# Bi-WKV gate and FFN on one core: the FFN's results of blocks 1 to 7 added up in DRAM by GpSimd's accumulating transfers

## The chip, the core and the metric

One core of a Trainium2 chip runs the whole kernel. The time is in device microseconds. Before the change it is 1723.0 us, the median of three runs (1722.13 to 1724.81).

## The reference

`x` and `fside` are (4, 1024, 1024), `cond` is (4, 256), all float32.

```python
r, k, v = x, fside, fside
tf = sigmoid(sum(time_emb)); decay = exp(-exp(w)) * (0.5 + 0.5 * tf)
ek = exp(min(k, 30)); ekv = ek * v
nf, df, nb, db = ...            # scans of ekv and ek over the sequence, forward and backward
base = sigmoid(r) * (nf + nb - ekv + euk * v) / max(df + db - ek + euk, 1e-8)
mix = base * (0.8 + 0.2 * tf)
h = mix @ W1.T                  # 4096 hidden columns
a = gelu(clip(round(h / 0.1)) * 0.1)
out = x + a @ W2.T
```

## The kernel before

The output is computed in eight blocks of 512 rows (`BLOCKS`), held transposed: eight tiles of 128 features by 512 rows (`CT` = `DT` = 8). A block has 8 hidden units `s` of 512 columns (`STEPS`) and 8 output tiles `d`. While TensorE works on block n, ScalarE and VectorE make the gate of block n + 1 (`tile_group`, and the four `part`s that `mix` calls in `chained_block`), and check the weights: 64 checks, each a load of 512 KB, a conversion to int8 on ScalarE (`check_i8`, L1258) and a comparison on VectorE (`check`, L1832); a check's load waits for the check before it (`load_check`, L524). Sixteen of them fall in block 7.

Block 0 multiplies plainly. Blocks 1 to 7 multiply in a scheme with 7 products instead of 8: an operand is cut in 2 x 2 quadrants, and the result's four quadrants are built up in PSUM banks by products named 1 to 7. ScalarE's `seed` (L1171) copies product 1 from one bank to the next, `spill_p5` (L1180) puts product 5 in `sp5`, and VectorE's `seed_u4` (L1714) sets up the bank for products 7 and 3: TensorE's `products_73` and `y_73` wait for it (`s_u4`). The hidden units use `products_15`, `products_73`, `products_26`, `product_4` (L810). The output of hidden units 0 to 3 is made in the same way in the middle of the block, in two parts `e` of four tiles: `y_15`, `y_73`, `y_26`, `y_4` (L875). Its results are quadrants `(e, c)`, c = 0 to 3, of 128 x 512. The order on TensorE there is: `y_15(0)`, `y_26(0)`, `y_15(1)`, `y_73(0)`, `y_26(1)`, `y_4(0)`, `products_15(5)`, `y_73(1)`, `products_26(5)`, `y_4(1)`. The output of hidden units 4 to 7 follows at the block's end, plainly, tile by tile (`output`, L956; the last tile of block 7 in two halves, `output_end`, L972).

Each engine's order is written out by hand, in `chained_block` of ScalarE and of VectorE and in `ffn_block` of SyncE. An engine that waits for a semaphore holds all that is behind it.

The results of blocks 1 to 7 go through four buffers `xy` of 128 x 512 in float32:

- Middle of the block: SyncE loads a quadrant of `x` (`load_quad`), VectorE adds the quadrant of PSUM to it (`y_quad`, L1734; for c = 3 also `sp5` before it, L1750), SyncE stores the sum in the DRAM array `y_part` (`store_quad`).
- End of the block: SyncE loads a tile of `y_part` (`residual`, L485), VectorE adds the tile of PSUM (`result`, L1812), SyncE stores it in `out` (`store`, L508). Two buffers take loads, two take stores. The last tile's halves are added by `result_end` (L1820, L1823).

Weights come through a ring of eight slots of 512 KB (`ring_load`, L457) on SyncE's queue, in line with all else that SyncE does. GpSimd issues the transfers that convert or copy weights, all in block 0 and before it (L717 to L728).

After the last check VectorE adds up the verdicts, one product on TensorE (L1028) makes a flag of them, and each engine reads it.

Of the kernel before, what the change touches and what calls it, by code (L numbers as in the profile page):

```python
# [5 lines left out]
P = 128  # L6
ALU = mybir.AluOpType
# [31 lines left out]
def adaln_ffn_kernel(nc, x, fside, cond, w, u, w1, w2, out):  # L39
# [22 lines left out]
    with ExitStack() as ctx:  # L62
# [12 lines left out]
        y_part = nc.dram_tensor("y_part", [BLOCKS, DT, P, T], F32).ap()  # L75
# [189 lines left out]
        s_y5 = sem("s_y5")  # L265
        s_xq = [sem(f"s_xq{k}") for k in range(4)]
        s_yq = [sem(f"s_yq{k}") for k in range(4)]
# [56 lines left out]
        def w1_pair(s, h):  # L324

            return (s // 2 + 2 * h, s % 2) if s < SPLIT else (s, h)

# [106 lines left out]
        def _(sp):  # L434
# [39 lines left out]
            def residual(n, d):  # L474
                k, uses = d % 2, DT // 2 * n + d // 2
                if uses > 0:
                    sp.wait_ge(s_res[k], uses)
                src = x[n % BLOCKS // 2, 1 - n % 2, d]
                if 0 < n < BLOCKS:
                    src = y_part[n, d]  # L480
                    sp.wait_ge(s_yq[2 * k], 16 * (2 * (n - 1) + d // 4 + 1))
                    sp.wait_ge(s_yq[2 * k + 1], 16 * (2 * (n - 1) + d // 4 + 1))
                    if d < 2:
                        sp.wait_ge(s_yq[k], 16 * 2 * n)
                sp.dma_start(x_in[:, k, :], src).then_inc(s_x[k], 16)  # L485

            def quad(dram, e, c):

                return dram[4 * e + c // 2:4 * e + 4:2, :, H * (c % 2):H * (c % 2 + 1)].rearrange("i p t -> p i t")

            def load_quad(n, e, c):
                if e == 1:
                    sp.wait_ge(s_yq[c], 16 * (2 * (n - 1) + 1))
                elif c < 2:
                    sp.wait_ge(s_res[c], DT // 2 * n)
                else:
                    sp.wait_ge(s_store[c - 2], 16 * DT // 2 * n)
                sp.dma_start(xy_quads[:, c, :, :], quad(x[n // 2, 1 - n % 2], e, c)).then_inc(s_xq[c], 16)

            def store_quad(n, e, c):  # L500
                done = (s_y11, s_y12, s_y21, s_c22)[c]
                sp.wait_ge(done, part_y(n, e) + 1 if c == 3 else 2 * (n - 1) + e + 1)
                sp.dma_start(quad(y_part[n], e, c), xy_quads[:, c, :, :]).then_inc(s_yq[c], 16)

            def store(n, d):
                k, uses = d % 2, DT // 2 * n + d // 2
                sp.wait_ge(s_res[k], uses + 1)
                sp.dma_start(out[n % BLOCKS // 2, 1 - n % 2, d], y_out[:, k, :]).then_inc(s_store[k], 16)  # L508

            def store_end(n, d):  # L510
                sp.wait_ge(s_resend, 1)
                sp.dma_start(out[n // 2, 1 - n % 2, d][:, 0:H], y_out[:, 1, 0:H]).then_inc(s_store[1], 16)
                sp.wait_ge(s_res[1], DT // 2 * n + d // 2 + 1)
                sp.dma_start(out[n // 2, 1 - n % 2, d][:, H:T], y_out[:, 1, H:T]).then_inc(s_store[1], 16)
# [62 lines left out]
            def ffn_block(n):  # L577
# [8 lines left out]
                for s in range(1, SPLIT + 1):  # L586
                    ring_load(3)
                    if s == 1:
                        store(n - 1, DT - 2)
                        store(n - 1, DT - 1)  # L590
# [4 lines left out]
                    if s == SPLIT:  # L595
                        for c in range(4):
                            load_quad(n, 0, c)
# [6 lines left out]
                store_quad(n, 0, 0)  # L604
                ring_load(3)
                load_quad(n, 1, 0)
# [4 lines left out]
                store_quad(n, 0, 3)  # L611
                store_quad(n, 0, 1)
                ring_load(2)
                store_quad(n, 0, 2)
                load_quad(n, 1, 3)
                load_quad(n, 1, 1)
                store_quad(n, 1, 0)
                ring_load(2)
                load_quad(n, 1, 2)
# [5 lines left out]
                store_quad(n, 1, 3)  # L625
                store_quad(n, 1, 1)
                load_check(at + 2 if nxt else at + 7)
                ring_load(2)
                store_quad(n, 1, 2)
# [10 lines left out]
                residual(n, 0)  # L640
                residual(n, 1)
# [4 lines left out]
                store(n, 0)  # L646
                residual(n, 2)
                ring_load(2)
                store(n, 1)
                residual(n, 3)  # L650
# [4 lines left out]
                store(n, 2)  # L655
                residual(n, 4)
# [4 lines left out]
                store(n, 3)  # L661
                residual(n, 5)
                load_check(at + 5 if nxt else at + 15)
                ring_load()
                store(n, 4)
                residual(n, 6)
                ring_load()
                store(n, 5)
                residual(n, 7)
# [7 lines left out]
            store(BLOCKS - 1, DT - 2)  # L677
            store_end(BLOCKS - 1, DT - 1)
            for k in range(2):
                sp.wait_ge(s_store[k], 16 * (DT // 2 * BLOCKS + k))  # L680
# [25 lines left out]
            with sp.If(needs_general > 0):  # L706
                for m in range(BLOCKS):
                    general_block(m)
                for k in range(2):
                    sp.wait_ge(s_store[k], 16 * (DT // 2 * 2 * BLOCKS + k))  # L710

        @block.gpsimd
        def _(pool):
# [9 lines left out]
            for s in range(STEPS):  # L723
                pool.wait_ge(s_y, 2 + s)
                for r, h, k in ((WP1, 0, 0), (WP2, 0, 1), (WP4, 1, 1)):
                    g, pair = w1_pair(s, h)
                    pool.wait_ge(s_w1cast[g], 16)
                    pool.dma_start(w1s[s][:, r, :, :], w1_quads[g][:, pair, :, k, :]).then_inc(s_w1copy[s], 16)  # L728
            for d in range(DT):
                pool.wait_ge(s_w2cast[d], 16)  # L730
            for s in range(STEPS):
                pool.wait_ge(s_w1copy[s], 16 * 3)

        @block.tensor
        def _(pe):
# [79 lines left out]
            def bank_free(n, s, q):  # L815
# [7 lines left out]
                if s == 0 and n > 1:  # L823
                    for k in range(2):
                        pe.wait_ge(s_res[k], DT // 2 * (n - 1) + 2)
                if s == 1 and n > 1:
                    for k in range(2):
                        pe.wait_ge(s_res[k], DT // 2 * n)
# [134 lines left out]
            def output_end(n, d):  # L963
# [3 lines left out]
                pe.wait_ge(s_res[0], DT // 2 * n + 2)  # L967
# [62 lines left out]
            def general_block(m):  # L1030
                n = BLOCKS + m
                pe.wait_ge(s_out, CT * (n + 1))
                for s in range(STEPS):
                    pe.wait_ge(g_w[s % 2], 16 * (DT * m + s // 2 + 1))
                    for j in range(FPS):
                        if FT * m + FPS * (s - 2) + j + 1 > 0:
                            pe.wait_ge(g_q, FT * m + FPS * (s - 2) + j + 1)
                        if s == 0 and j in (0, 3):
                            pe.wait_ge(s_res[j % 2], DT // 2 * n)
# [4 lines left out]
                for d in range(DT):  # L1044
                    pe.wait_ge(g_w[d % 2], 16 * (DT * m + STEPS // 2 + d // 2 + 1))
                    pe.wait_ge(s_res[d % 2], DT // 2 * n + d // 2)
# [16 lines left out]
        def _(act_e):  # L1063
# [186 lines left out]

            def check_i8(at):
# [53 lines left out]
            def chained_block(n, nxt, g0, at):  # L1305
# [42 lines left out]
                act_hi(n, SPLIT, 1)  # L1348
                seed(part_y(n, 1))
                check_i8(at if nxt else at + 3)  # L1350
                spill_p5(part_y(n, 1))
                if nxt:
                    tile_group_between(g0 + 3)
                check_i8(at + 1 if nxt else at + 4)
# [4 lines left out]
                else:  # L1359
                    check_i8(at + 5)  # L1360
                quantise11(n, SPLIT + 1)

# [39 lines left out]
                check_i8(at + 2 if nxt else at + 10)  # L1402
                if nxt:
                    tile_group_between(g0 + 7)
                    operands_hi(n + 1, 1)
                check_i8(at + 3 if nxt else at + 11)
                check_i8(at + 4 if nxt else at + 12)
                if nxt:
                    reciprocal(g0 + 7, s_gate, g0 + 8)
                    operands_hi(n + 1, 2)  # L1410
                    if n + 2 < BLOCKS:
                        tile_group(g0 + CT)
                    operands_hi(n + 1, 3)
                check_i8(at + 5 if nxt else at + 13)
                if not nxt:
                    check_i8(at + 14)
                    check_i8(at + 15)

# [54 lines left out]
        def _(dve):  # L1473
# [256 lines left out]
            def y_quad(n, e, c, ps, done, flag_of):  # L1730

                dve.wait_ge(done, part_y(n, e) + 1)
                dve.wait_ge(s_xq[c], 16 * (2 * (n - 1) + e + 1))
# [465 lines left out]
```

## Time and profile before

| | |
|---|---|
| median of three runs | 1723.0 us |
| the profiled execution | 1722.96 us |
| its span | 1720.6 us |
| granted TensorE clock, mean | 0.991 of full speed |
| TensorE busy | 1647.8 us, 96% |
| VectorE busy | 1298.0 us, 75% |
| ScalarE busy | 936.3 us, 54% |
| GpSimd busy | 24.7 us, 1% |
| moved by DMA | 376.97 MB, queues busy 67.4% of 16 engines |

The profiled execution is one run; its span leaves out what lies ahead of the first and behind the last instruction, 2.4 us. A matmul's mean time is from its start to its modelled end, and matmuls overlap: busy time over count is their pace. Blocks 1 to 7 begin at about 288, 490, 693, 897, 1102, 1304 and 1508 us. A part of the chain called "issue" is time in which an engine waited for nothing that the profile shows.

### The profile page before, as it was taken

To read this page: it belongs to the slowest core of one execution; us is meant where nothing else is said; L and a number is where in the kernel's file an instruction comes from. 1 tells how busy PE (TensorE), PEld (TensorE's weight loads), DVE (VectorE), ACT (ScalarE), POOL (GpSimd) and SP (SyncE) were. 2 spreads that over 40 slices of the span, in tenths; PEclk is the share of its full clock that TensorE was granted. 3 is DMA by queue.
4 is the path that set the end of the run, shared out by engine and by line. 5 is a ranking of instruction groups with operands and counts; after the bars stand their busy time and mean duration, and the time that the engine had idled before them with its cause. 6 is when DMAs were issued, how large, how long until landed. Compare 5 with 4: busy or idle time off the path is not lost. (4 is left out here: it accounts for less than half of the span.)

```text
span 1720.6 us, 30810 instructions
## 1 busy us (share of the span) xinstructions
PE 1647.8 (96%) x12258; PEld 1200.1 (70%) x12258; DVE 1298.0 (75%) x1795; ACT 936.3 (54%) x1461; POOL 24.7 (1%) x44
## 2 busy tenths in 40 slices
PE   1699999999999999999999999999999999999997
PEld 0244445888578884888758885688857887488864
DVE  8988896887779769788697877888787876955232
ACT  3578332765656564673836646475555646365141
POOL 0000110000000000000000000000000000000000
PEclk9799999999999999999999999999999999999999
DMA  8979885587375865668466684757737585565754
GB/s 238 245 176 281 307 305 166 180 275 238 135 275 167 273 204 207 217 193 285 152 222 227 221 262 137 265 184 268 242 133 272 172 283 178 199 213 187 247 181 152
DMA packets 153461, 376.97 MB, mean 219 GB/s; under 512 B 15328, under 2 KB 44256, under 8 KB 152800
## 3 DMA queue, kind: packets, MB, share of 16 engines
q1 hardware_dynamic: 150624, 351.86, 61.0%
q0 software_dynamic: 2688, 23.07, 5.9%
q8 instruction: 99, 1.62, 0.4%
q14 instruction: 50, 0.41, 0.1%
HBM read 347.61 MB, written 67.11 MB: 241 GB/s over the span
## 5 line engine op out<-in xcount | busy, mean ns | idle before, releaser
L810 PE MATMUL ps<-mo,w_ring 128*128 128x256 f16 x6272 | 695.4, 273 | 5.9 <-DVE q L1726 4.0
L810 PEld LDWEIGHTS ps<-mo,w_ring 128*128 128x128 f16 x6272 | 612.9, 98 | 83.7 <-issue 7.9
L956 PE MATMUL ps<-act,w_ring 128*128 128x512 f16 x1760 | 383.3, 379 | 0.0
L875 PE MATMUL ps<-act,w_ring 128*128 128x256 f16 x3136 | 348.1, 273 | 0.0
L875 PEld LDWEIGHTS ps<-act,w_ring 128*128 128x128 f16 x3136 | 306.3, 98 | 36.0
L956 PEld LDWEIGHTS ps<-act,w_ring 128*128 128x128 f16 x1760 | 172.2, 98 | 203.2
L1768 DVE SCALAR_TENSOR_TENSOR act<-a,act 128x1024 f16<-128x1024 f32 x72 | 87.8, 1221 | 86.4 <-ACT act L1232 86.4
L1222 ACT ACTIVATE a<-q 128x1024 f32<-128x1024 int16 x124 | 131.0, 1057 | 7.0 <-DVE act L1768 2.0
L1171 ACT ACTIVATE ps<-ps 128x512 f32<-128x512 f32 x70 | 40.7, 581 | 169.0 <-PE ps L810 113.7
L751 PE MATMUL ps<-mo,w_ring 128*128 128x512 f16 x256 | 66.4, 427 | 56.3 <-DMA w_ring<-w_half 33.6
L1714 DVE SCALAR_TENSOR_TENSOR ps<-sp,ps 128x512 f32<-128x512 f32 x70 | 48.5, 692 | 85.3 <-issue 37.3
L942 PE MATMUL ps<-act,w_ring 128*128 128x512 f16 x512 | 110.7, 379 | 0.0
L1258 ACT ACTIVATE q<-tt 128x1024 int8<-128x1024 f32 x48 | 50.5, 1051 | 109.7 <-DMA tt<-in_w_dram 109.7
L751 PEld LDWEIGHTS ps<-mo,w_ring 128*128 128x128 f16 x256 | 27.1, 108 | 95.1 <-issue 47.1
L942 PEld LDWEIGHTS ps<-act,w_ring 128*128 128x128 f16 x512 | 50.1, 98 | 60.4
L1616 DVE SCALAR_TENSOR_TENSOR ND<-EE,bonus,ND 128x1024 f32<-128x1024 f32 x64 | 81.8, 1279 | 1.6
L1596 DVE TENSOR_TENSOR_SCAN ND<-decay,back,ND 128x512 f32<-128x512 f32 x64 | 81.9, 1280 | 0.6
L1600 DVE TENSOR_TENSOR_SCAN ND<-decay,back,ND 128x512 f32<-128x512 f32 x64 | 81.7, 1276 | 0.0
L1107 ACT ACTIVATE RCP<-ND 128x512 f32<-128x512 f32 x64 | 40.3, 630 | 67.1 <-DVE ND L1620 64.7
L1232 ACT ACTIVATE act<-a 128x1024 f16<-128x1024 f32 x72 | 75.9, 1054 | 1.5
L1779 DVE TENSOR_TENSOR tt<-a 128x1024 f32<-128x1024 f32 x28 | 34.3, 1225 | 54.2 <-ACT a L1222 54.2
L1204 ACT ACTIVATE q<-ps 128x512 int16<-128x512 f32 x56 | 33.3, 595 | 70.1 <-PE ps L810 69.9
(129 smaller groups left out, 1730.1 us busy)
## 6 DMA issues: line engine op xcount, KB each, us to landing
w_ring<-w1s SPq DMA_DIRECT2D x168, 512.0 KB, 4.6
w_ring<-w_half SPq DMA_DIRECT2D x130, 512.0 KB, 5.2
w_ring<-w2s SPq DMA_DIRECT2D x56, 512.0 KB, 5.1
tt<-in_w_dram SPq DMA_DIRECT2D x48, 512.0 KB, 5.6
V<-in_fside_dram SPq DMA_DIRECT2D x64, 256.0 KB, 5.7
R<-in_x_dram SPq DMA_DIRECT2D x64, 256.0 KB, 5.9
w_half<-in_w_dram POOLq DMA_DIRECT2D x16, 1024.0 KB, 9.5
xy<-in_x_dram SPq DMA_DIRECT2D x64, 256.0 KB, 5.0
```

The source lines that it names most:

```text
L751: mm = pe.matmul(bank[4 * (s % 2) + j][:, :], w1_ring[:, slots[2 * s + j // 2], j % 2, c, :], mix0[:, c, p, :], start=(first and p == 0), ...
L810: mm = pe.matmul(dst[:, f, :], wp_ring[:, k, r, f, q, :], mo[:, op, q, p, :], start=(fresh and f == 0 and q == 0 and p == 0), stop=(q == K ...
L875: mm = pe.matmul(dst[:, i, :], wy_ring[:, k, i, 2 * s + j, :], ao[:, s, op, j, p, :], start=(fresh and i == 0 and s == 0 and j == 0 and p ...
L942: mm = pe.matmul(y_ps[y][:, :], w2_ring[:, k, f, :], act[:, FPS * s + j, p, :], start=(h == 0 and f == 0 and p == 0), stop=(h == 1 and f = ...
L956: mm = pe.matmul(bank[d][:, :], w2_ring[:, k, FPS * (s - SPLIT) + j, :], act[:, act_at(n, s) + j, p, :], start=(s == SPLIT and j == 0 and ...
L1222: sc.activation(a32[:, 2 * h:2 * h + 2, :], src[:, s % 2, 2 * h:2 * h + 2, :], ACT.Gelu_apprx_tanh, scale=QSTEP).then_inc(s_gelu, 1)
L1232: sc.activation(act[:, f:f + 2, 0, :], a32[:, 2 * h:2 * h + 2, :], ACT.Copy, scale=ACT_SCALE).then_inc(s_ahi, 1)
L1258: sc.activation(small, full, ACT.Copy, scale=W_SCALE).then_inc(s_chki8, 1)
L1596: v.tensor_tensor_scan(DEN[:, k, :][:, ::-1], dec(b, c), DEN[:, k, :][:, ::-1], back[:, k, 1:2], ALU.mult, ALU.add).then_inc(s_dbwd, 1)
L1600: v.tensor_tensor_scan(NUM[:, k, :][:, ::-1], dec(b, c), NUM[:, k, :][:, ::-1], back[:, k, 0:1], ALU.mult, ALU.add).then_inc(s_nbwd, 1)
L1616: v.scalar_tensor_tensor(out=ND[:, k, :, :], in0=EE[:, k, :, :], scalar=bonus[:, b, c:c + 1], in1=ND[:, k, :, :], op0=ALU.mult, op1=ALU.ad ...
L1768: v.scalar_tensor_tensor(out=act[:, f:f + 2, 1, :], in0=a32[:, 2 * h:2 * h + 2, :], scalar=ACT_SCALE, in1=act[:, f:f + 2, 0, :], op0=ALU.m ...
```

## The change

`y_part` is gone. For blocks 1 to 7:

- SyncE copies `x` to `out` in DRAM, four transfers of two tiles each (`copy_x`), one in each of hidden units 1 to 4.
- ScalarE copies the quadrants 0 to 2 of each part from PSUM to an `xy` buffer (`y_quad`), and later the output tiles (`output_out`), the last tile of block 7 excepted. VectorE makes quadrant 3 from PSUM and `sp5` in one instruction (`y22`).
- GpSimd adds each buffer to `out` in DRAM by a transfer with `accum_op=ALU.add`, in the order of `event`: (0,0), (0,3), (0,1), (1,0), (0,2), (1,3), (1,1), (1,2), then the tiles. Tiles begin when all eight quadrants have landed.
- All four buffers are used in turn. Whoever fills one waits until the transfer from it has landed (`buffer_free`, `s_acc`).
- TensorE waits for ScalarE's copies (`s_ev`) before it reuses the banks of the output, where it waited for VectorE's `s_res`.
- The last tile of block 7 stays with VectorE: SyncE loads it from `out` after tile 5's transfer has landed, since it uses tile 5's buffer (`residual_end`).

```diff
+        def buffer_free(engine, n, i):
+            if added(n, i) > 0:
+                engine.wait_ge(s_acc[i % 4], 16 * added(n, i))
...
+            def copy_x(n, i):
+                sp.dma_start(out[n // 2, 1 - n % 2, 2 * i:2 * i + 2], x[n // 2, 1 - n % 2, 2 * i:2 * i + 2]).then_inc(s_xcopy, 16)
...
+            def residual_end(n, d):
+                for k in range(4):
+                    sp.wait_ge(s_acc[k], 16 * added(n, 8))
+                sp.wait_ge(s_acc[1], 16 * (added(n, 2 * DT - 3) + 1))
+                sp.dma_start(x_in[:, 1, :], out[n // 2, 1 - n % 2, d]).then_inc(s_x[1], 16)
...
+            for n in range(1, BLOCKS):
+                dram = out[n // 2, 1 - n % 2]
+                pool.wait_ge(s_xcopy, 16 * 4 * n)
+                for e, c in ((0, 0), (0, 3), (0, 1), (1, 0), (0, 2), (1, 3), (1, 1), (1, 2)):
...
+                    pool.dma_start(quad(dram, e, c), xy_quads[:, k, :, :], accum_op=ALU.add).then_inc(s_acc[k], 16)
+                for k in range(4):
+                    pool.wait_ge(s_acc[k], 16 * added(n, 8))
+                for d in range(DT if n + 1 < BLOCKS else LAST):
+                    pool.wait_ge(s_ev, DT * (n - 1) + d + 1)
+                    pool.dma_start(dram[d], xy[:, d % 4, :], accum_op=ALU.add).then_inc(s_acc[d % 4], 16)
...
-                    for k in range(2):
-                        pe.wait_ge(s_res[k], DT // 2 * (n - 1) + 2)
+                    pe.wait_ge(s_ev, DT * (n - 2) + DT // 2)
...
+            def y_quad(n, e, c):
+                i, q = event(e, c), part_y(n, e)
+                act_e.wait_ge((s_p2, s_p3, s_p4)[c], q + 1)
+                buffer_free(act_e, n, i)
+                sc.activation(xy_quads[:, i % 4, :, :], halves[4 * (q % 2) + (0, 3, 1)[c]], ACT.Copy,
+                              scale=1.0 / QUAD_SCALE).then_inc((s_y11, s_y12, s_y21)[c], 1)
+
+            def output_out(n, *tiles):
+                for d in tiles:
+                    act_e.wait_ge(s_y, y_all(n, d))
+                    buffer_free(act_e, n, DT + d)
+                    sc.activation(xy[:, d % 4, :], bank[d][:, :], ACT.Copy, scale=1.0 / ACT_SCALE).then_inc(s_ev, 1)
...
                 spill_p5(part_y(n, 1))
+                y_quad(n, 0, 1)
                 if nxt:
                     tile_group_between(g0 + 3)
+                y_quad(n, 1, 0)
+                y_quad(n, 0, 2)
                 check_i8(at + 1 if nxt else at + 4)
...
-            def y_quad(n, e, c, ps, done, flag_of):
-
-                dve.wait_ge(done, part_y(n, e) + 1)
```

ScalarE, middle of block 2, before (L1258 is the check's conversion, L1171 a seed, L1180 a spill, L1090 to L1113 a tile of the next block's gate):

```order
L1171 ACTIVATE ps<-ps 128x512 [waits s_q21,s_p1]
L1258 ACTIVATE q<-tt 128x1024 [waits s_chk,s_gelu,s_chkload]
L1180 ACTIVATE sp<-ps 128x512 [waits s_c22,s_p5]
L1125 ACT_TABLE_LOAD
L1090 ACTIVATE EE,ksum<-V 128x512 [waits s_gate,s_v1]
L1099 ACTIVATE RCP,vsum<-V 128x512 [waits s_vsq,s_out]
L1107 ACTIVATE RCP<-ND 128x512 [waits s_out,s_vsq,s_gate]
L1109 ACTIVATE RCP<-RCP 128x512 [waits s_ln]
L1113 ACTIVATE R,rsum<-R 128x512 [waits s_r1]
L1258 ACTIVATE q<-tt 128x1024 [waits s_chk,s_gelu,s_chkload]
L1171 ACTIVATE ps<-ps 128x512 [waits s_y21,s_p1]
```

and now:

```order
L1257 ACTIVATE xy<-ps 128x512 [waits s_acc0,s_p2]
L1172 ACTIVATE ps<-ps 128x512 [waits s_q21,s_p1]
L1273 ACTIVATE q<-tt 128x1024 [waits s_chk,s_gelu,s_chkload]
L1181 ACTIVATE sp<-ps 128x512 [waits s_c22,s_p5]
L1257 ACTIVATE xy<-ps 128x512 [waits s_acc2,s_p3]
L1126 ACT_TABLE_LOAD
L1091 ACTIVATE EE,ksum<-V 128x512 [waits s_gate,s_v1]
L1100 ACTIVATE RCP,vsum<-V 128x512 [waits s_vsq,s_out]
L1108 ACTIVATE RCP<-ND 128x512 [waits s_out,s_vsq,s_gate]
L1110 ACTIVATE RCP<-RCP 128x512 [waits s_ln]
L1114 ACTIVATE R,rsum<-R 128x512 [waits s_r1]
L1257 ACTIVATE xy<-ps 128x512 [waits s_acc3,s_p2]
L1257 ACTIVATE xy<-ps 128x512 [waits s_acc0,s_p4]
L1273 ACTIVATE q<-tt 128x1024 [waits s_chk,s_gelu,s_chkload]
L1172 ACTIVATE ps<-ps 128x512 [waits s_y21,s_p1]
```

The copies (L1257) of quadrants (1,0) and (0,2) stand between the tile's gate and the second conversion (L1273).

VectorE at the same place, now (L1845 is the check, L1746 `seed_u4` of part 1):

```order
L1580 TENSOR_TENSOR EE<-EE,V 128x512 [waits s_ekx]
L1608 SCALAR_TENSOR_TENSOR ND<-decay,EE 128x512 [waits s_ekv]
L1610 SCALAR_TENSOR_TENSOR ND<-decay,EE 128x512
L1586 TENSOR_TENSOR ND<-ND,RCP 128x512 [waits s_rcp0]
L1621 COPY back<-carry 128x2 [waits s_carry,s_dfwd,s_nfwd]
L1845 SCALAR_TENSOR_TENSOR tt,bad<-q,tt 128x1024 [waits s_chki8]
L1746 SCALAR_TENSOR_TENSOR ps<-sp,ps 128x512 [waits s_q12,s_p6,s_sp5]
```

Before, the sum of quadrant (1,0) stood between the check and the seed; the check was ahead of the seed then too.

ScalarE at the end of block 7, now (before, seven conversions stood here with nothing between them):

```order
L1264 ACTIVATE xy<-ps 128x512 [waits s_acc2,s_y]
L1273 ACTIVATE m_st<-m_st 128x1024 [waits s_chk,s_chkload]
L1264 ACTIVATE xy<-ps 128x512 [waits s_acc3,s_y]
L1273 ACTIVATE m_st<-m_st 128x1024 [waits s_chk,s_chkload] x2
L1264 ACTIVATE xy<-ps 128x512 [waits s_acc0,s_y]
L1264 ACTIVATE xy<-ps 128x512 [waits s_acc1,s_y]
L1264 ACTIVATE xy<-ps 128x512 [waits s_acc2,s_y]
```

Tiles 4, 5 and 6 are copied after the last conversion.

## Rows read from the trace of the kernel before

**Rows 1.** The page's busy us (share of the span) and instructions of each engine.

```profile
PE 1647.8 (96%) x12258; PEld 1200.1 (70%) x12258; DVE 1298.0 (75%) x1795; ACT 936.3 (54%) x1461; POOL 24.7 (1%) x44
```

**Rows 2.** Waits of TensorE: engine, line, who was waited for: us, times, longest us.

```profile
PE ps L810 <- DVE q L1726: 4.0, 5, 0.9
...
PE ps L810 <- ACT ps L1171: 1.7, 2, 1.4
```

**Rows 3.** Chain of waits, around the start of block 6: start us, us, what.

```profile
1313.72 5.23 DMA tt<-in_w_dram
...
1334.48 0.70 DVE q L1726
1335.17 0.14 issue
```

**Rows 4.** Groups by line: line engine op, out<-in xcount | busy us, mean ns | idle before.

```profile
L1812 DVE SCALAR_TENSOR_TENSOR xy<-ps,xy 128x512 f32<-128x512 f32 x63 | 42.9, 685 | 15.3 <-PE ps L942 8.2 <-DMA xy<-y_part 7.0
...
L1734 DVE SCALAR_TENSOR_TENSOR xy<-ps,xy 128x512 f32<-128x512 f32 x56 | 38.3, 688 | 25.5 <-PE ps L875 18.6 <-issue 3.6 <-DMA xy<-in_x_dram 2.8
...
L1750 DVE SCALAR_TENSOR_TENSOR xy<-sp,xy 128x512 f32<-128x512 f32 x14 | 9.6, 688 | 22.5 <-DMA xy<-in_x_dram 22.5
```

**Rows 5.** Timeline of TensorE, middle of block 7: start us, us, instructions.

```profile
1582.70 24.62 PE L875 MATMUL ps<-act,w_ring 128*128 128x256 f16 x224
1607.15 3.66 PE L810 MATMUL ps<-mo,w_ring 128*128 128x256 f16 x32
1610.65 7.15 PE L875 MATMUL ps<-act,w_ring 128*128 128x256 f16 x64
```

**Rows 6.** Timeline of VectorE in the same stretch.

```profile
1597.48 1.22 DVE L1832 SCALAR_TENSOR_TENSOR m_st<-m_st 128x1024 f32<-128x1024 int8 x1
...
1603.92 0.70 DVE L1714 SCALAR_TENSOR_TENSOR ps<-sp,ps 128x512 f32<-128x512 f32 x1 [1.69 <-PE ps L875]
1607.35 0.69 DVE L1734 SCALAR_TENSOR_TENSOR xy<-ps,xy 128x512 f32<-128x512 f32 x1 [2.74 <-PE ps L875]
```

**Rows 7.** Timeline of ScalarE, block 7, hidden units.

```profile
1536.75 1.05 ACT L1258 ACTIVATE m_st<-m_st 128x1024 int8<-128x1024 f32 x1
...
1540.97 0.58 ACT L1171 ACTIVATE ps<-ps 128x512 f32<-128x512 f32 x1
1541.47 1.05 ACT L1242 ACTIVATE act<-a 128x1024 f16<-128x1024 f32 x1
```

**Rows 8.** Timeline of VectorE, block 7, hidden units.

```profile
1537.83 1.23 DVE L1832 SCALAR_TENSOR_TENSOR m_st<-m_st 128x1024 f32<-128x1024 int8 x1 [1.82 <-ACT m_st L1258]
...
1538.98 0.69 DVE L1714 SCALAR_TENSOR_TENSOR ps<-sp,ps 128x512 f32<-128x512 f32 x1
```

**Rows 9.** DMA issues: out<-in, queue, xcount, KB each, median us from issue to landing.

```profile
w_half<-in_w_dram POOLq DMA_DIRECT2D x16, 1024.0 KB, 9.5
...
out_dram<-xy SPq DMA_DIRECT2D x63, 256.0 KB, 4.7
...
w1s<-w_half POOLq DMA_DIRECT2D x24, 256.0 KB, 6.4
```

**Rows 10.** The page's 40 slices of 43 us, VectorE: busy tenths.

```profile
DVE  8988896887779769788697877888787876955232
```

**Rows 11.** Timeline of GpSimd, block 0: three issues in one row.

```profile
192.03 2.09 POOL L728 DMA_DIRECT2D w1s<-w_half  x3 [40.95 <-PE ps L942]
```

**Rows 12.** Chain of waits at the program's end.

```profile
1682.30 4.71 DMA m_st<-in_w_dram
...
1711.23 2.99 DMA xy<-y_part
```

**Rows 13.** Timeline of the last 60 us, three engines.

```profile
1678.61 1.23 DVE L1832 SCALAR_TENSOR_TENSOR m_st<-m_st 128x1024 f32<-128x1024 int8 x1 [5.11 <-ACT m_st L1258]
...
1702.66 7.15 PE L972 MATMUL ps<-act,w_ring 128*128 128x256 f16 x64
...
1707.83 1.06 ACT L1258 ACTIVATE m_st<-m_st 128x1024 int8<-128x1024 f32 x1 [5.83 <-DMA m_st<-in_w_dram]
```

More of the change, by code:

```diff
@@ L264, in adaln_ffn_kernel @@
         s_y21 = sem("s_y21")
-        s_y5 = sem("s_y5")
-        s_xq = [sem(f"s_xq{k}") for k in range(4)]
-        s_yq = [sem(f"s_yq{k}") for k in range(4)]
+        s_xcopy = sem("s_xcopy")
+        s_acc = [sem(f"s_acc{k}") for k in range(4)]
+        s_ev = sem("s_ev")
         s_yend = sem("s_yend")
@@ L326, in w1_pair, with uses_of, quad, event @@
             return (s // 2 + 2 * h, s % 2) if s < SPLIT else (s, h)
+        def uses_of(n, d):
+            if n == 0:
+                return d // 2
+            return DT // 2 if n < BLOCKS else DT // 2 * (n - BLOCKS + 1) + d // 2 + d % 2
+        def quad(dram, e, c):
+            return dram[4 * e + c // 2:4 * e + 4:2, :, H * (c % 2):H * (c % 2 + 1)].rearrange("i p t -> p i t")
+        def event(e, c):
+            return ((0, 0), (0, 3), (0, 1), (1, 0), (0, 2), (1, 3), (1, 1), (1, 2)).index((e, c))
+        def added(n, i):
+            return 4 * (n - 1) + i // 4
+        def buffer_free(engine, n, i):
+            if added(n, i) > 0:
+                engine.wait_ge(s_acc[i % 4], 16 * added(n, i))
+            elif i % 4 < 2:
+                engine.wait_ge(s_res[i % 4], DT // 2)
+            else:
+                engine.wait_ge(s_store[i % 4 - 2], 16 * DT // 2)
         def quantised0(s, j):
@@ L587, in ffn_block @@
                     ring_load(3)
-                    if s == 1:
-                        store(n - 1, DT - 2)
-                        store(n - 1, DT - 1)
+                    if n == 1 and s == 1:
+                        store(0, DT - 2)
+                        store(0, DT - 1)
+                    copy_x(n, s - 1)
                     if not nxt:
@@ L732, in _ @@
                 pool.wait_ge(s_w1copy[s], 16 * 3)
+            for k in range(4):
+                pool.wait_ge(s_acc[k], 16 * (added(BLOCKS - 1, 2 * DT) - k // 3))
         @block.tensor
@@ L823, in bank_free @@
                 if s == 0 and n > 1:
-                    for k in range(2):
-                        pe.wait_ge(s_res[k], DT // 2 * (n - 1) + 2)
+                    pe.wait_ge(s_ev, DT * (n - 2) + DT // 2)
                 if s == 1 and n > 1:
-                    for k in range(2):
-                        pe.wait_ge(s_res[k], DT // 2 * n)
+                    pe.wait_ge(s_ev, DT * (n - 1))
             def products_15(n, s):
```

172 lines of the change are left out of this document (58 added, 114 removed).

## The prediction

> **What bounds the kernel now.** I read the busy shares first. TensorE is busy for 1647.8 of 1720.6 us, VectorE for 1298.0, ScalarE for 936.3 [rows 1]. So work taken from VectorE is worth something only where TensorE waits for it. The list of TensorE's waits says how much that is: in blocks 1 to 7, 4.0 us for `quantise22` on VectorE (five times) and 1.7 us for a `seed` on ScalarE [rows 2], 5.7 us together. The chain of waits shows what stands behind them: a check load of 5.23 us near the start of block 6, then some 16 us of ScalarE and VectorE work, then `quantise22`, 0.14 us later the product [rows 3]. No eviction to `xy` is in that chain. Blocks 1 to 7 thus run at TensorE's pace, and only the last microseconds of the program, where the last tile waits for a load, lie elsewhere [rows 12].
>
> **What is removed.** VectorE loses 55 of its 63 evictions of 685 ns, the 56 quadrant sums of 688 ns become 14, and 14 additions of the spill, two per block, go [rows 4]: (55 + 42 + 14) x 0.69 = 77 us of busy time. Price on the path: 0, since the cover is TensorE and none of the waits of [rows 2] stands behind these instructions. It stays 0 also if VectorE comes earlier by that much, for `quantise22` waits for the check load and ScalarE. SyncE loses 56 loads and 56 stores of quadrants, 55 loads of partial sums and 55 stores of results, and gets 28 copies of 512 KB (four each in the stretch of hidden units 1 to 4). They stand ahead of weight loads on SyncE's queue, which run up to seven chunks of 3.5 us ahead; price 0.
>
> **What ScalarE gets.** 42 quadrants and 55 tiles, 0.50 us from start to start [rows 7], 49 us on an engine that is 54% busy. The share does not matter, the order does: each copy waits in line, and what stands behind it waits too. Two of the new waits are long. The copy of quadrant (0,1) holds ScalarE until `y_73` of part 0 is through; the next tile's exponentials then come some 6 us later, and VectorE has that much to give. The copy of quadrant (0,2) is the one that counts. It needs the end of `y_4` of part 0, and behind it stands a check conversion; VectorE's check waits for that conversion; behind the check stands `seed_u4` of part 1; and TensorE's next but one piece, `y_73` of part 1, needs that seed.
>
> I time it in block 7. `y_4` ends at 1607.15, and `y_73` starts at 1610.65 [rows 5]. An engine that waited for `y_4` starts 0.20 us after it, 1607.35 [rows 6]. Copy, to the next start: 0.50 [rows 7]. Conversion: 1.05 [rows 7], and 0.03 from its end to the check [rows 7, 8]. Check to the next start: 1.15 [rows 8]. Seed: 0.69 [rows 8]. Release of TensorE: 0.14 [rows 3]. That is 1607.35 + 3.56 = 1610.91, so TensorE waits 0.26 us. Before, the check had run at 1597.48 and the seed at 1603.92, 6.7 us ahead of its use [rows 6]. The same order stands in all seven blocks: 7 x 0.26 = **+1.8 us**. The bounds are 0 (the pieces overlap a little more) and 0.5 x 7 = 3.5.
>
> **The output tiles.** Tile 0's copy stands ahead of a tile's exponentials and holds them until the tile's product is through; VectorE, rid of its evictions there, makes that up before the next block's operands are due. The copies of tiles 6 and 7 fall in time in which ScalarE waits for the next block's first product. Price 0; if that cover is gone, TensorE would wait at the start of a block, up to 0.5 us per copy.
>
> **The buffers.** Four buffers serve 16 transfers per block. The closest reuse is of the buffer of quadrant (0,3): the end of its product is 96 of 224 matmuls into the stretch at 1582.70, 1593.2, and (1,3)'s is 3.5 us after 1610.65, 1614.1: 20.9 us. Unless a transfer takes that long, nobody waits for one. No row shows an accumulating transfer. The nearest is the one of GpSimd with the same size and a DRAM target, 6.4 us from issue to landing; the ends are a plain store of the same buffer, 4.7, and a transfer four times as large, 9.5 [rows 9]. I take 6.4. The issue costs GpSimd 0.70 us, a third of 2.09 [rows 11].
>
> A rule speaks against this. Those three issues of 2.09 us [rows 11] lie in the fifth of the 40 slices, where VectorE was 8 tenths busy [rows 10], and they are not drawn out. The Trainium skill (SBUF — State Buffer, section "SBUF: two separate sides") says that GpSimd can't write descriptors while VectorE runs an instruction in a two-port mode, and so such a transfer waits. Trace and rule do not conflict: the instructions beside these transfers have two tensor inputs, and the page names plain copies and `tensor_scalar`. If the rule bit, a transfer would be late by one VectorE instruction, about 1.2 us, which changes only the end.
>
> **The end.** Before, SyncE issued the load of check 12 only at 1682.30, since the stores of tiles 0 and 1 stood ahead of it [rows 12]; the check before it had ended at 1678.61 + 1.23 = 1679.84 [rows 13]. Now it goes there at once: the chain of checks comes 2.45 us sooner, and the last conversion starts at 1707.83 - 2.45 = 1705.38 [rows 13]. But ScalarE copies tiles 4, 5 and 6 only behind it: 1706.44, 1706.94, 1707.44. Tile 4 is ready for GpSimd at 1707.02, its issue takes 0.70, tile 5 is issued at 1707.72 and lands 6.4 later, 1714.1. The last load waits for it (same buffer), takes 2.99 as before [rows 12] and lands at 1717.1, where it landed at 1714.2. The end is the same from there: **+2.9 us**, with a transfer of 4.7 us +1.2, with one of 9.5 us +6.0. TensorE ends at 1709.8 [rows 13] and is not what ends last.
>
> The Trainium skill (DMA: Bandwidth & Descriptors, section "Anatomy of one DMA") gives 2.0 us plus the bytes over 436 GB/s; by that page my estimate for 256 KB is 2.6 us; the end would come to -0.9 instead of +2.9, and the sum to 1723.9, which is the case "hidden altogether" below. The rows have plain transfers of that size at 4.7 and more beside other traffic, so the forecast goes by them.
>
> **Sum:** 1.8 + 2.9 = +4.7 us on 1722.96, the time of the profiled execution, which is the median of the runs (1723.0) within 0.1: **1727.7 us**. The case's own range is +1.2 (no wait in the middle, 4.7 us transfers) to +9.5 (0.5 us per block, 9.5 us transfers).
>
> **Rivals.**
> - *Hidden altogether.* The 0.26 us is a difference of 3.76 and 3.50; a little overlap cancels it, and a transfer of 4.7 us leaves +1.2: 1724.2.
> - *Faster.* The waits of 5.7 us [rows 2] go, if less traffic lets the check load land sooner than 5.23 us. SyncE has fewer transfers in line, which speaks for it; that the loads right ahead of it are tile loads and weights, which stay, speaks against it. 1723.0 - 5.7 + 1.2 = 1718.5.
> - *Crowded.* GpSimd's transfers of tiles 6 and 7 fly just before the check load of the next block. The waits of [rows 3] grow with its landing one to one: 1 us later in each of six blocks gives 1727.7 + 6 = 1733.7.
> - *Slow additions,* the one that ends far on the other side. Adding means that DRAM is read, then written. From about 21 us per transfer on, ScalarE waits for a buffer at quadrant (0,2), and every further microsecond is paid in seven blocks and once at the end. At 25 us: 1723.0 + 1.8 + 7 x 3.9 + 2.9 + (25 - 6.4) = 1773.6. No row shows a 256 KB transfer near that.
>
> **How the numbers follow.** A measurement of this kernel can tell about 0.2%, 3.4 us, from no change. Chances: forecast 0.50, hidden 0.20, faster 0.12, crowded 0.10, slow additions 0.08. Of the forecast's 0.50, three tenths lie below +3.4. Slower: 0.35 + 0.10 + 0.08 = 0.53. Same: 0.15 + 0.20 = 0.35. Faster: 0.12. The range of 8 in 10 leaves out the slow additions and about half of the faster case and reaches past the crowded one: 1720 to 1737; the forecast's own range is 1724.2 to 1732.5.
>
> **What would show it.** A new wait of TensorE for VectorE's `seed_u4` at `y_73` of part 1, seven times, 0.2 to 0.5 us each; VectorE idle some 6 us before the check ahead of it, released by ScalarE; landing of 5 to 9 us for the accumulating transfers; no wait of ScalarE for one; at the end GpSimd's issue for tile 5 near 1709.5 (1707.7 plus the 1.8), the load behind it, then two half tiles. Wrong is the forecast if ScalarE waits for accumulating transfers inside the blocks, if TensorE's 5.7 us vanish, or if the last load comes before 1711.

## The result and the profile after

| | before | after |
|---|---|---|
| median of 10 runs each, in turn on one chip | 1722.92 us | 1727.99 us |
| lowest and highest | 1721.71, 1724.81 | 1725.66, 1732.71 |
| profiled execution, its span | 1722.96, 1720.6 us | 1728.37, 1726.6 us |
| ratio, 95% interval | | 1.003 (1.0022 to 1.0038) |

The kernel is 5.1 us (0.3%) slower; 4.7 had been forecast. The experiments show that the number came out right although two effects that the sum had put at 0 are missing in it. One is the crowding of the DMA engines, which costs 5.8 to 13.4 us. The other is VectorE's relief, which gives 2.4 to 10.0 us back. Each depends on whether the other is there, and both together cost 3.4 us. (The comparisons leave disturbed executions out; the held additions below had two, at 2518 and 6646 us, among ten.)

The page of the changed kernel, busy us of each engine and its DMA queues, answers to [rows 1]:

```profile
PE 1648.9 (96%) x12258; PEld 1199.1 (69%) x12258; DVE 1232.5 (71%) x1684; ACT 986.4 (57%) x1558; POOL 139.2 (8%) x155
...
q1 hardware_dynamic: 105216, 308.33, 52.8%
q0 software_dynamic: 25840, 52.18, 17.8%
```

VectorE lost 65.5 us, where 77 had been forecast: 0.59 for each of the 111 instructions taken (their durations are 0.69, and each overlaps its neighbour by 0.1); ScalarE got 50.1, 49 had been forecast. The queues of the kernel before:

```profile
q1 hardware_dynamic: 150624, 351.86, 61.0%
q0 software_dynamic: 2688, 23.07, 5.9%
```

GpSimd's queue (q0) moves 29 MB more in 111 additions and takes 307 us of the 16 DMA engines (17.8% of 1726.6) where it took 102: 1.85 us of all 16 for each addition of 262 KB. (The page counts the time that a queue's packets took. In some windows below this share comes out above 1, so packets overlap in it.) SyncE's queue (q1) needs 138 us less (61.0% of 1720.6 before, 52.8% of 1726.6 now).

The waits of TensorE in blocks 1 to 7, which answer to [rows 2] (L813 is the line of the hidden units' products, L876 that of the part products):

```profile
PEld ps L813 <- issue: 7.1, 8, 1.2
PE ps L813 <- DVE q L1758: 2.7, 3, 0.9
PEld ps L876 <- issue: 2.5, 7, 0.4
PE ps L813 <- ACT ps L1172: 2.2, 3, 1.0
```

At the starts of blocks TensorE waits 4.9 us in sum (5.7 before), and there are seven new waits at L876. The page puts these on the weight loads (PEld) and names no releaser; that it is the seed follows from the times below. The middle of block 7, timelines of TensorE, ScalarE and VectorE, answers to [rows 5] and [rows 6]:

```profile
1608.49 3.66 PE L813 MATMUL ps<-mo,w_ring 128*128 128x256 f16 x32
1612.25 7.15 PE L876 MATMUL ps<-act,w_ring 128*128 128x256 f16 x64
...
1608.69 0.60 ACT L1257 ACTIVATE xy<-ps 128x512 f32<-128x512 f32 x1 [6.39 <-PE ps L876]
1609.18 1.05 ACT L1273 ACTIVATE m_st<-m_st 128x1024 int8<-128x1024 f32 x1
...
1610.26 1.23 DVE L1845 SCALAR_TENSOR_TENSOR m_st<-m_st 128x1024 f32<-128x1024 int8 x1 [14.80 <-ACT m_st L1273]
1611.41 0.69 DVE L1746 SCALAR_TENSOR_TENSOR ps<-sp,ps 128x512 f32<-128x512 f32 x1
```

From the start of the 32 matmuls to that of the 64 it is 3.76 us, where it was 3.50: 0.26. It is 3.76 or 3.77 in all seven blocks. Copy, conversion, check and seed stand behind each other as forecast, and the 64 matmuls start 0.15 us after the seed's end at 1612.10.

The chain of waits at the end, which answers to [rows 12]:

```profile
1704.11 3.80 DMA m_st<-in_w_dram
1707.93 0.02 ACT m_st L1273
...
1708.90 0.59 ACT xy L1264
1709.48 0.28 issue
1709.77 0.54 POOL out_dram L729
1710.31 6.49 DMA out_dram<-xy
...
1716.88 3.03 DMA xy<-out_dram
1719.93 0.42 DVE xy L1833
```

The last sum starts at 1719.93 instead of 1714.24, 5.7 us later.

### The profile page after: what moved, and what is told of

Read it like the earlier page. It is cut to its first block and busy times, and to the rows that moved or that the text cites. A ratio compares the mean times of both kernels' runs of the same rounds, so it can differ in the third digit from the quotient of the medians.

```text
span 1726.6 us, 30636 instructions
## 1 busy us (share of the span) xinstructions
PE 1648.9 (96%) x12258; PEld 1199.1 (69%) x12258; DVE 1232.5 (71%) x1684; ACT 986.4 (57%) x1558; POOL 139.2 (8%) x155
## 3 DMA queue, kind: packets, MB, share of 16 engines
q1 hardware_dynamic: 105216, 308.33, 52.8%
q0 software_dynamic: 25840, 52.18, 17.8%
## 5 line engine op out<-in xcount | busy, mean ns | idle before, releaser
L813 PE MATMUL ps<-mo,w_ring 128*128 128x256 f16 x6272 | 695.1, 273 | 5.1 <-DVE q L1758 2.7
L813 PEld LDWEIGHTS ps<-mo,w_ring 128*128 128x128 f16 x6272 | 613.1, 98 | 82.5 <-issue 7.1
L876 PE MATMUL ps<-act,w_ring 128*128 128x256 f16 x3136 | 348.1, 273 | 0.7
L876 PEld LDWEIGHTS ps<-act,w_ring 128*128 128x128 f16 x3136 | 305.8, 98 | 38.4 <-issue 2.5
L724 POOL DMA_DIRECT2D out_dram<-xy x56 | 66.9, 1195 | 810.6 <-ACT xy L1257 709.6
L1746 DVE SCALAR_TENSOR_TENSOR ps<-sp,ps 128x512 f32<-128x512 f32 x70 | 48.4, 692 | 110.2 <-issue 49.4
L1273 ACT ACTIVATE q<-tt 128x1024 int8<-128x1024 f32 x48 | 50.4, 1049 | 77.0 <-DMA tt<-in_w_dram 77.0
L943 PEld LDWEIGHTS ps<-act,w_ring 128*128 128x128 f16 x512 | 50.1, 98 | 60.4
L729 POOL DMA_DIRECT2D out_dram<-xy x55 | 47.6, 883 | 544.1 <-ACT xy L1264 539.0
L1257 ACT ACTIVATE xy<-ps 128x512 f32<-128x512 f32 x42 | 24.7, 588 | 112.0 <-PE ps L876 112.0
L1845 DVE SCALAR_TENSOR_TENSOR tt<-q,tt 128x1024 f32<-128x1024 int8 x48 | 58.6, 1221 | 35.0 <-ACT q L1273 34.9
```

What stands on the lines that cost most here:

```text
L724: pool.dma_start(quad(dram, e, c), xy_quads[:, k, :, :], accum_op=ALU.add).then_inc(s_acc[k], 16)
L813: mm = pe.matmul(dst[:, f, :], wp_ring[:, k, r, f, q, :], mo[:, op, q, p, :], start=(fresh and f == 0 and q == 0 and p == 0), stop=(q == K ...
L876: mm = pe.matmul(dst[:, i, :], wy_ring[:, k, i, 2 * s + j, :], ao[:, s, op, j, p, :], start=(fresh and i == 0 and s == 0 and j == 0 and p ...
L943: mm = pe.matmul(y_ps[y][:, :], w2_ring[:, k, f, :], act[:, FPS * s + j, p, :], start=(h == 0 and f == 0 and p == 0), stop=(h == 1 and f = ...
L1845: v.scalar_tensor_tensor(out=full, in0=small, scalar=1.0 / W_SCALE, in1=full, op0=ALU.mult, op1=ALU.not_equal, accum_out=bad[:, at:at + 1] ...
```

## The experiments

All edits are made to the changed kernel. The "starts" in a sentence below are TensorE's waits for VectorE and ScalarE in the hidden units of blocks 1 to 7, in us (lines L810 to L816, by the kernel). The runs were made on three chips, each beside the kernel before, whose median was 1722.7, 1723.6 and 1722.7 us. The changed kernel itself was not run again beside them, so a difference from its 1728.0 can be off by about 1 us; the ratios to the kernel before do not suffer from this.

**ScalarE's order in the middle.**

```diff
+                check_i8(at + 1 if nxt else at + 4)
                 y_quad(n, 1, 0)
                 y_quad(n, 0, 2)
-                check_i8(at + 1 if nxt else at + 4)
```

> Only ScalarE's order in the middle of blocks 1 to 7 is changed: the check's conversion stands ahead of the copies of quadrants (1,0) and (0,2). My theory: VectorE's check and seed_u4 of part 1 come back ahead of their use, TensorE's wait of 0.26 us before y_73 of part 1 is gone in all seven blocks, and the time falls by 1.8 us from 1728.0 to 1726.2. Rival, the loss in the middle has nothing to do with this order (slower transfers, a longer block 0): the gap stays, and the time stays at 1728.0.

1724.6 us (ratio to before 1.001, 1.0001 to 1.0019): 3.4 less than with the change. The seven waits at L876 are gone, and the 3.76 us are 3.50 again in all seven blocks. The other half of the gain is open, and the two intervals are wide enough to hold 1.8 as well as 3.4. The starts of its profiled execution, the slowest with 1729.07 us, are 7.8 and so more than the changed kernel's 4.9.

```profile
PE ps L813 <- DVE q L1758: 4.3, 5, 0.9
PE ps L813 <- ACT ps L1172: 3.5, 3, 2.0
```

The next run has 3.2, and neither edit touches the start of a block: the starts vary from one execution to the next, and so does the start of block 1, which lies between 286.9 and 289.5 us in the profiled executions of this document.

**The end of block 7.**

```diff
                 output_out(n, 3)
+                if not nxt:
+                    output_out(n, 4, 5)
                 check_i8(at + 4 if nxt else at + 14)
...
                 else:
+                    output_out(n, 6)
                     check_i8(at + 15)
-                    output_out(n, 4, 5, 6)
```

> Only the last block's order on ScalarE is changed: tiles 4 and 5 are copied before check conversion 14, tile 6 before conversion 15, where all three stood behind 15. My theory: tile 5's transfer is issued near 1699 instead of 1710.3 and has landed long before the last load is needed; the last two half tiles then follow TensorE and the verdict sums, near 1712 instead of 1720, so the time falls by about 8 us from 1728.0 to 1720. Rival, the chain of checks sets the end whatever the copies do: the last check ends near 1710.2 as now, and with the flag behind it less than 3 us are gained, 1725 or more. Second rival, the additions ahead in the queue are what is slow: the landing moves by less than the issue.

1720.45 us (0.9988, 0.9979 to 0.9997), as expected: 7.5 us are the price of three copies of 0.5 us that stand behind two conversions, which wait for loads. Now the last check and the verdict sums set the end, and the last sum starts at 1709.54. GpSimd's last issue, which started at 1710.9 in the changed kernel, is at 1701.34:

```profile
1701.34 0.86 POOL L729 DMA_DIRECT2D out_dram<-xy  x1 [6.05 <-ACT xy L1264]
```

With this edit alone the kernel is some 2 us faster than before.

**Ballast on VectorE.** It gets back as much work as the change took, 111 maxima of 128x512 over a constant table, 0.6 us from start to start, at the places of the removed instructions. It reads a table in SBUF and waits for no load, so it gives back the work and not the waits of the old instructions for `x` and `y_part`:

```diff
+            def ballast(times=1):
+                for _ in range(times):
+                    dve.wait_ge(s_bal, bal[0])
+                    bal[0] += 1
+                    v.reduce_max(verdict[:, 12:13], RAMP[:, :], AX_X).then_inc(s_bal, 1)
```

> VectorE gets 16 maxima over 128 x 512 of SBUF per block (15 in block 7), about 0.6 us each, at the places where its evictions and quadrant sums stood before, the one between the check and seed_u4 of part 1 put behind the seed; nothing uses them. My theory: VectorE's relief is worth nothing, so the time stays within 1.5 us of 1728.0 and TensorE's waits stay at 7 us or so in blocks 1 to 7. Rival, the relief had bought back part of the loss: the time rises by 3 us or more.

1737.98 us (1.0084, 1.007 to 1.0098): 10 us more than the changed kernel (9.3 by the ratios), where the forecast's reason says 0. The waits of TensorE in that run:

```profile
PEld ps L814 <- issue: 17.3, 10, 3.4
PE ps L814 <- ACT ps L1173: 11.0, 5, 3.1
PE ps L814 <- DVE q L1759: 3.6, 4, 0.9
```

The starts are 14.6. What may cause this is seen at the start of block 2: SyncE's first issue there, which loads a check, waits until VectorE's last check of block 1 has left the buffer `tt`, and every weight load stands behind it on the queue. The issues are at 493.24 before, 491.00 after the change and 492.56 with ballast. Then a burst follows, 4.4 MB until 506 in the changed kernel (GB/s of its 2 us windows, added up). DMA share and GB/s in 2 us windows (start:end us, sum, busy of each engine, clock, DMA share, GB/s), first the changed kernel:

```profile
492.00:494.00 2.00, 2.00 (x21) 1.80 (x19) 0.00 (x0) 0.68 (x2) 0.86 (x1) 1.00 0.94 119
494.00:496.00 2.00, 2.00 (x21) 1.79 (x20) 0.00 (x0) 0.60 (x1) 0.00 (x0) 1.00 1.01 346
496.00:498.00 2.00, 2.00 (x21) 1.79 (x19) 0.00 (x0) 1.54 (x2) 0.00 (x0) 1.00 1.04 347
498.00:500.00 2.00, 2.00 (x21) 1.79 (x19) 1.46 (x2) 0.00 (x0) 0.00 (x0) 1.00 1.08 316
```

and the kernel before:

```profile
496.00:498.00 2.00, 2.00 (x21) 1.79 (x20) 0.52 (x1) 0.85 (x1) 0.00 (x0) 1.00 0.99 387
498.00:500.00 2.00, 2.00 (x21) 1.80 (x19) 1.93 (x4) 1.27 (x3) 0.00 (x0) 1.00 1.02 414
500.00:502.00 2.00, 2.00 (x21) 1.80 (x19) 1.89 (x3) 0.60 (x1) 0.00 (x0) 1.00 1.02 397
```

The 16 DMA engines are busy in both, but at first 119 and then 316 to 347 GB/s move where 387 to 414 did: GpSimd's additions of tiles 6 and 7, issued at 490.30 and 492.39, run inside the burst. (The page counts the same bytes for additions and for plain stores, so whatever an addition reads of its target is not in these figures.) The next check load (issued at 499.50 before, at 500.40 in the two others) has its bytes behind all of these, and ScalarE's conversion of it starts at

```profile
504.61 1.06 ACT L1258 ACTIVATE q<-tt 128x1024 int8<-128x1024 f32 x1 [3.10 <-DMA tt<-in_w_dram]
```

before, with the change and with ballast at

```profile
504.89 1.06 ACT L1273 ACTIVATE q<-tt 128x1024 int8<-128x1024 f32 x1 [2.31 <-DMA tt<-in_w_dram]
```

```profile
507.65 1.06 ACT L1274 ACTIVATE q<-tt 128x1024 int8<-128x1024 f32 x1 [5.96 <-DMA tt<-in_w_dram]
```

So a new theory: VectorE's relief starts the burst 2.2 us earlier (491.00 for 493.24), the additions make it about as much longer, and the two cancel. The runs up to here fit it and do not show it; the held additions below test it.

**The check ahead of the seed** on VectorE, so that the second check load is issued sooner:

```diff
-                seed_u4(hid(n, 0))
                 if n > 1:
                     check(at - 2)
+                seed_u4(hid(n, 0))
```

> Only VectorE's order at the start of blocks 2 to 7 is changed: the check stands ahead of seed_u4 instead of behind it. My theory: the waits of 0.3 to 1.0 us for the seed of unit 2 and for quantise22 near the start of a block hang on the next check's load, which is issued when this check ends; it now goes out 1.5 to 2 us sooner, these waits (4.9 us in the profiled execution) shrink below 2 us, and the time falls by 3 to 4 us to about 1724.5. Rival, ScalarE and VectorE are simply full there: the load lands sooner but the waits stay, 1728.0.

1727.88 us (1.0025, 1.0015 to 1.0036), no change. The load is issued 1.3 us sooner, and ScalarE's conversion, released by it, starts no sooner:

```profile
499.09 0.33 SPq L536 DMA_DIRECT2D tt<-in_w_dram  x1
...
505.23 1.06 ACT L1273 ACTIVATE q<-tt 128x1024 int8<-128x1024 f32 x1 [2.95 <-DMA tt<-in_w_dram]
```

In the mean of blocks 2 to 7, counted from the block's start, this load is issued 1.2 us sooner and its conversion starts at 14.4 us in both. In a full burst an earlier issue did not bring the bytes sooner, which fits the new theory and not the one that this run was made for.

**Held additions.** GpSimd keeps tiles 6 and 7 back until VectorE's first quantisation of the next block, at about 505:

```diff
                     pool.wait_ge(s_ev, DT * (n - 1) + d + 1)
+                    if d == 6 and n + 1 < BLOCKS:
+                        pool.wait_ge(s_c22, hid(n + 1, 0) + 1)
```

> The changed kernel, with GpSimd's additions of tiles 6 and 7 of blocks 1 to 6 held back until VectorE's first quantisation of the next block (some 14 us later). Crowding theory: at the start of a block the two additions fall into the burst of weight and check loads (the DMA engines are fully busy at 316 to 347 GB/s where they moved 387 to 414 before), which costs the check load some 2 to 3 us; without them the TensorE waits at the starts of blocks fall from 4.9 us in sum to 0 to 2, and the time to 1724 us. VectorE theory (the burst is as it was, and only VectorE's and ScalarE's own order counts): no change, 1728 us.

> The same hold of the additions, and VectorE loaded with the 111 maxima of the earlier experiment that measured 1738.0 us. Crowding theory: the ballast costs because the burst starts later and is longer too; with the additions out of the burst the block starts as it did before the change, 1728 us (1726 to 1731). VectorE theory: the ballast costs its 10 us in any case, 1738 us.

> The changed kernel with VectorE loaded only at the output tiles (eight maxima per block, seven in the last; none at the quadrants in the middle). Crowding theory: all of the cost comes from VectorE's reaching the check at the end of a block 1.6 to 2.8 us later, so as with all 111: 1737 us (1734 to 1740). VectorE theory (its load in the middle counts too): half of it, 1733 us.

> The changed kernel with both additions made plain stores by GpSimd; the adding of x and of the partial sums to the output is left out. Crowding theory: a 256 KB store takes the DMA engines for less than an addition does, so the waits of TensorE at the starts of blocks fall from 4.9 us to 0 to 2 and the last landing from 6.5 us to some 4.5: 1728 - 4 - 2 = 1722 us. If adding costs nothing over storing: 1728 us, with the landing at 6 us and over.

Measured, with the starts of each profiled execution:

| | median us | ratio to before (95%) | starts |
|---|---|---|---|
| kernel before | 1722.9 | | 5.7 |
| changed kernel | 1728.0 | 1.003 (1.0022 to 1.0038) | 4.9 |
| held additions | 1722.2 | 0.9994 (0.9983 to 1.0004) | 0.9 |
| held, with ballast | 1724.6 | 1.0008 (0.9998 to 1.0018) | 4.5 |
| ballast alone | 1738.0 | 1.0084 (1.007 to 1.0098) | 14.6 |
| ballast at the output tiles only | 1740.5 | 1.0096 (1.0077 to 1.0115) | 13.8 |
| plain stores | 1716.0 | 0.9958 (0.9941 to 0.9975) | 0.9 |

The held additions give 5.8 us (6.2 by the ratios). Ballast costs 10.0 without the hold and 2.4 with it (9.3 and 2.4 by the ratios), though VectorE's work is the same; and half of the ballast, at the output tiles, costs no less than all: its 1740.5 is even above what had been expected, 1734 to 1740. So beside a load at the output tiles, what VectorE does in the middle costs nothing that these runs show, and its work around the block's last checks is worth 10 us beside a crowded burst and 2.4 beside one that is not. The crowding theory had 1728 (1726 to 1731) for the run with both, which came out under that, at 1724.6. In the run with the hold the same stretch reads

```profile
492.00:494.00 2.00, 2.00 (x21) 1.78 (x19) 0.00 (x0) 0.58 (x1) 0.00 (x0) 1.00 0.91 297
494.00:496.00 2.00, 2.00 (x21) 1.79 (x19) 0.00 (x0) 1.59 (x3) 0.00 (x0) 1.00 1.03 410
496.00:498.00 2.00, 2.00 (x21) 1.79 (x19) 0.25 (x1) 0.55 (x1) 0.00 (x0) 1.00 1.00 384
498.00:500.00 2.00, 2.00 (x20) 1.79 (x19) 2.00 (x4) 0.56 (x1) 0.00 (x0) 1.00 0.82 275
```

with the engines no longer full from 498 on.

Block 2 is one of six. The means of blocks 2 to 7, each time counted from TensorE's first product of the block, say the same (one profiled execution of each kernel, times from its timelines):

| | first check load issued | conversion of the second load | block 2 to block 7 |
|---|---|---|---|
| kernel before | 2.1 | 14.6 | 1017.4 |
| changed kernel | -0.4 | 14.4 | 1017.6 |
| ballast alone | 1.1 | 16.3 | 1028.9 |
| held additions | -0.6 | 13.3 | 1012.8 |
| held, with ballast | 1.3 | 13.9 | 1016.9 |

The change brings the first load forward by 2.5 us and the conversion by only 0.2; the hold brings the conversion 1.1 us forward with the first load about where it was. A late first load moves the conversion by 1.9 us beside the additions and by 0.6 without them. The ballast takes back 1.5 of the 2.5 us, so it is not quite VectorE as it was.

The plain stores leave the adding out, and so do not compute the result. They went 6 us below what had been expected of them. Their queue line and their chain at the end:

```profile
q0 software_dynamic: 11568, 52.18, 10.3%
...
1702.80 2.72 DMA out_dram<-xy
1705.60 3.04 DMA xy<-out_dram
```

The same bytes take 177 us of the DMA engines instead of 307: (177 - 102) / 111 = 0.68 us per store against 1.85 per addition, with 80 packets for each against 209. GpSimd's issue falls from 0.86 to 0.54 us per tile and from 1.19 to 0.72 per pair of quadrant halves, and the last landing from 6.49 to 2.72 us; my 4.5 was still too much. With that the last load starts at 1705.60; in the held kernel, whose starts are the same, it is 1711.14. The check loads of this last chain are shorter too (4.03, 4.10, 4.32 and 3.92 us where the held kernel has 5.16, 5.13, 5.24 and 3.89), so the additions crowd the loads of block 7 as well: 3.5 of the 5.5 us between these two last loads are the landing, and 2.0 lie ahead of it.

**Both good edits, without and with the middle.** The same diffs as above, put together.

> The changed kernel with two edits: tiles 4 to 6 of block 7 copied ahead of the last two check conversions (alone it measured 1720.5 us), and the additions of tiles 6 and 7 of blocks 1 to 6 held out of the burst of loads at the next block's start (alone 1722.2 us). If the two are independent, their gains of 7.5 and 5.8 us add up: 1728.0 - 7.5 - 5.8 = 1714.7 us (1713 to 1717). If both ease the same thing (the DMA engines as a whole), less: 1718 us or more.

> The same two edits, and ScalarE's conversion of the check (at + 1) put ahead of its copies of quadrants (1,0) and (0,2) in the middle of every block. Middle theory as forecast: seven waits of TensorE of 0.26 us go, 1.8 us less than without this edit: 1713 us. Rival: the earlier 3.4 us of this edit alone came from the starts of blocks, which the hold now covers, and the seven waits of 0.26 us are only moved: within 0.7 us of the run without it.

1716.3 us (0.9962, 0.9948 to 0.9976) and 1712.8 us (0.9943, 0.993 to 0.9957). The first came 1.6 us above the sum of the single gains, inside the expected range and less than its interval is wide: the gains add up as far as this can tell. The second is 3.4 us below it, where the middle edit alone had given 3.4. Its profile shows 1.8 of these: the waits at L876 (`2.5, 7, 0.4` by the weight loads' issue) are gone, and the pieces with the wait are shorter in the chain, first without the middle edit, then with it:

```profile
1402.97 7.15 PE ps L878 x64
...
1605.22 7.15 PE ps L878 x64
```

```profile
1403.62 6.99 PE ps L878 x64
...
1605.60 6.99 PE ps L878 x64
```

From block 6 to block 7 it is 201.98 us instead of 202.25. What the other 1.6 are is open; the five runs of each spread over 4.5 and 2.4 us, and an interval of 0.14% is 2.4 us. The starts are 0.9 in both, as in every profiled execution without additions in the burst or with plain ones, except that with ballast. The last version is 9.9 us faster than the kernel before and the best that was run.

## Why the prediction was right, and where it was not

**The middle, +1.8 us: right.** 0.26 us, seven times, by the very instructions named. Taking the wait out gave 3.4 us both times, so 1.8 may be low; this is still inside the bounds of 0 to 3.5, and the rows show no more than the 0.26 us.

**The end, +2.9 us: right in its mechanism.** The last sum is 5.7 us late where 4.7 (with the middle's 1.8) was forecast. (Block 1 began 0.8 us later in this execution, at 289.06 for 288.26, and the starts are 0.8 us shorter; these two cancel.) The addition took 6.49 us for 6.4 and the last load 3.03 for 2.99. That 6.4 fitted was luck: it was borrowed from a plain transfer within DRAM, and a plain store in the addition's place landed in 2.72. Tile 5's issue had been forecast near 1709.5 and began at 1710.31. The difference of 1 us between 5.7 and 4.7 lies mostly ahead of the addition: the last conversion started at 1707.93 and not at 1705.38 + 1.8 = 1707.2, since the check loads in the chain took 5.15, 5.04, 5.15 and 3.80 us, where [rows 12] had 4.71 and the two behind it took 4.56 and 4.59. The experiment on the end shows what this order costs, 7.5 us.

The estimate from the Trainium skill (DMA: Bandwidth & Descriptors, section "Anatomy of one DMA"), 2.6 us for 256 KB, agrees with the plain store that landed in 2.72 us and not with the additions: 6.49 for tile 5 behind tile 4's, and 3.8 for the quickest of all. Of the other rule, that VectorE keeps GpSimd from writing descriptors (SBUF — State Buffer, "SBUF: two separate sides"), no run here shows a trace. The issues of the tiles have a median of 0.86 us and a shortest of 0.86; two at the program's end stand out with 1.20 and 1.55, each of which began while the one before was still being issued. The prediction had misread its rows here: while the three issues of [rows 11] ran, VectorE ran nothing at all (from 190.76 to 198.18). Rows of the kernel before bear the conclusion out all the same, since the next three issues fell beside `TENSOR_TENSOR` instructions and took no longer:

```profile
198.79 0.68 DVE L1700 TENSOR_TENSOR sp<-w_ring 128x1024 f16<-128x1024 f16 x1
198.93 2.05 POOL L728 DMA_DIRECT2D w1s<-w_half  x3 [4.82 <-PE ps L942]
```

**GpSimd's issue, 0.70 us: too low.** It is 0.86 for a tile and 1.19 for quadrants. This is off the path but at the end, where GpSimd begins 0.28 us after tile 4's copy and tile 5's issue 0.54 behind that: 0.82 us for 0.70. **The buffers: right.** No wait of ScalarE for an addition; the 111 landed in 3.8 to 10.6 us, far from 21.

**"It stays 0 also if VectorE comes earlier": wrong.** This is the step that failed. It followed `quantise22` back to the check load and stopped there, as though the load's own start and length were given. Its landing is set by the burst in which it lies, and the burst starts when VectorE's last check of the block before frees the buffer of the load at the head of SyncE's queue. At the start of block 2 VectorE has lost three evictions of 0.69 us and a wait of 0.74 us for `y_part` ahead of that check, and the load goes out 2.2 us earlier. With VectorE's work given back as ballast the changed kernel takes 1738.0 us.

**The crowded rival, 0.10: it had happened.** It names tiles 6 and 7 ahead of the check load, and 1 us in each of six blocks; the hold brings the conversion 1.1 us forward in the mean of the six and gives 5.8 us back. That the time the additions occupy is what counts, and not their number, the plain stores show: they lie in the burst too, and the starts are 0.9. But it was set beside the forecast as another outcome, and its sign, longer waits at the starts, did not show, because the relief took the same away. Of the two missing terms the four runs make a square:

| | VectorE relieved | not relieved (ballast) |
|---|---|---|
| additions in the burst | 1728.0 | 1738.0 |
| additions held | 1722.2 | 1724.6 |

From the lower right corner, which has neither, crowding costs 13.4 us and the relief beside it gives 10.0 back; the other way round, the relief gives 2.4 and crowding costs 5.8. Either way 3.4 us are left. That corner should have the forecast's two terms alone, +4.7 on the kernel before. By its comparison it has +1.4 (1.0008, at most 1.0018, which is +3.1); by the profiled executions, of which the first was the slowest of its ten, 1726.14 - 1722.96 = +3.2 with starts 1.2 shorter, so +4.4. Where between these the truth lies is open, and with it how much of the forecast's +4.7 is its own two terms. Why crowding costs a VectorE that comes late so much more is seen in the means above (1.9 us on the conversion against 0.6) and not explained. That the two missing effects nearly cancelled was luck, and the reason given for each being 0 was wrong.

## What to carry to other kernels

A wait that ends with a DMA's landing is not the end of the trace back: look at what the queue's first transfer waited for, and at which bytes share the engines with it. When a transfer is moved to another queue, price its time on the DMA engines where the engines are full, and hold it back if its result is not needed there. Put an instruction that somebody waits for ahead of one that itself waits for a load: three copies of 0.5 us cost 7.5 us behind two such waits.

## What the runs showed of the hardware

An accumulating transfer of 262 KB from SBUF to DRAM took 1.85 us of all 16 DMA engines by packet time, 2.7 times a plain one by the same engine (0.68). It landed after 6.2 us in the median of the 111, against 3.6 for the plain ones (at the end of the program 6.49 against 2.72), and its issue took 0.86 us against 0.54. The forecast had a price for the landing and none for the time occupied. And in a stretch in which the DMA engines are full, a load issued 1.3 us sooner landed no sooner.
